# Grouped-query attention: stacked bf16 scores on the whole array against float32r scores in four row tiles

## The reference

```python
q = einsum('bsd,ed->bse', x, Wq).reshape(b, s, 32, 8).transpose(0, 2, 1, 3)
k = einsum('bsd,ed->bse', x, Wk).reshape(b, s, 8, 8).transpose(0, 2, 1, 3)
v = einsum('bsd,ed->bse', x, Wv).reshape(b, s, 8, 8).transpose(0, 2, 1, 3)
q, k = _apply_rope(q, k, s)
scores = jnp.einsum('bkgqd,bkld->bkgql', qg, k) * SCALE     # 1024 x 1024 a head
attn = jax.nn.softmax(scores, axis=-1)
out = jnp.einsum('bkgql,bkld->bkgqd', attn, v)
return jnp.einsum('bsd,ed->bse', out, Wo)
```

## Time and profile before

| | |
|---|---|
| median of 3 runs | 4268.53 us (4267.6 to 4272.98) |
| the profiled execution's own time | 4277.08 us |
| its span from the first to the last instruction | 4275.2 us |
| busy in the span | PE 86%, PEld 65%, DVE 62%, ACT 55%, POOL 18% |
| mean granted clock of PE | 0.944 |

### The profile page before, as it was taken

One profiled execution on the slowest core, in us unless ns is written; L12 is line 12 of the kernel. 1 busy time (PEld: TensorE's weight loads), 2 busy tenths in 40 slices (PEclk: granted clock), 3 DMA queues, 4 the chain that ended last, 5 costly groups with the idle time before them and its releaser, 6 DMA issues. The chain is left out here.

```text
span 4275.2 us, 66025 instructions
## 1 busy us (share of the span) xinstructions
PE 3696.2 (86%) x22804; PEld 2783.1 (65%) x22804; DVE 2636.4 (62%) x5009; ACT 2338.6 (55%) x4937; POOL 762.4 (18%) x864
## 2 busy tenths in 40 slices
PE   7999999992969969658888888886989999999979
PEld 6999999991848858312222222234878888988967
DVE  5666666666336653357666676633378888888853
ACT  5777677773413324126666666652256666766632
POOL 2233433220003410100000000002022323232200
PEclk9999999995989989859999999997989999999989
DMA  1000000000000000020000000002011011101010
GB/s 57 21 21 11 21 21 21 21 1 30 0 17 2 0 3 0 16 54 9 15 15 15 15 8 15 15 3 103 4 51 40 26 40 36 33 33 41 26 60 20
DMA packets 24580, 100.25 MB, mean 23 GB/s; under 512 B 5316, under 2 KB 6084, under 8 KB 18036
## 3 DMA queue, kind: packets, MB, share of 16 engines
q1 hardware_dynamic: 24356, 97.25, 7.0%
HBM read 84.52 MB, written 12.32 MB: 23 GB/s over the span
## 5 line engine op out<-in xcount | busy, mean ns | idle before, releaser
L1420 ACT ACTIVATE ga5m_pr<-ga5m_E 128x512 f32<-128x512 f32 x1024 | 582.2, 596 | 309.5 <-PE ga5m_E L1342 301.1
L1435 DVE TENSOR_REDUCE ga5m_nm<-ga5m_M 128x1 f32<-128x1024 f32 x512 | 597.9, 1218 | 179.4 <-PE ga5m_M L1328 178.9
L352 POOL TENSOR_TENSOR all_X<-all_X,at_part 128x512 f32<-128x512 f32 x256 | 335.2, 1309 | 996.0 <-ACT at_part L532 996.0
L1342 PE MATMUL ga5m_E<-ga5m_Q,ga5m_K 128*128 128x512 bf16 x1024 | 390.3, 393 | 65.8 <-ACT ga5m_pr L1420 51.8
L1328 PE MATMUL ga5m_M<-ga5m_K,ga5m_Q 128*128 128x512 bf16 x1024 | 323.9, 400 | 127.9 <-DMA ga5m_Q<-in_zrows 70.7
L417 PE MATMUL at_A<-all_ident,at_prob 128*128 128x128 f32 x2304 | 340.3, 274 | 30.2 <-ACT at_prob L540 20.9
L1342 PEld LDWEIGHTS ga5m_E<-ga5m_Q,ga5m_K 128*128 128x128 bf16 x1024 | 97.5, 98 | 405.4 <-ACT ga5m_pr L1420 346.9
L417 PEld LDWEIGHTS at_A<-all_ident,at_prob 128*128 128x128 f32 x2304 | 265.1, 140 | 59.0 <-DVE at_q1l L600 25.5
L616 DVE TENSOR_TENSOR at_pT1l<-at_A,at_pT1h 128x512 fp32r<-128x512 f32 (+1 forms) x384 | 235.6, 641 | 64.7 <-ACT at_pT1h L521 58.1
L1355 PE MATMUL ga5m_O<-ga5m_pr,ga5m_Vu 128*32 128x512 f32 x2048 | 270.9, 607 | 0.0
L1328 PEld LDWEIGHTS ga5m_M<-ga5m_K,ga5m_Q 128*128 128x128 bf16 x1024 | 88.5, 99 | 273.6 <-DVE ga5m_nm L1435 133.8
(11 more groups left out here) (328 smaller groups left out, 10660.7 us busy)
## 6 DMA issues: line engine op xcount, KB each, us to landing
at_raw<-in_pack SPq DMA_DIRECT2D x32, 1027.0 KB, 5.6
at_slope<-in_slopes SPq DMA_DIRECT2D x32, 512.0 KB, 4.1
ga5m_Q<-ga_qs SPq DMA_DIRECT2D x48, 192.0 KB
ga_qs<-ga5s_part SPq DMA_DIRECT2D x6, 512.0 KB
ga5m_K<-ga_ks SPq DMA_DIRECT2D x48, 48.0 KB
all_X<-in_x SPq DMA_DIRECT2D x1, 2048.0 KB, 7.2
tq_raw<-in_gu SPq DMA_DIRECT2D x1, 2048.0 KB, 7.6
hw_wug<-in_ug SPq DMA_DIRECT2D x1, 2048.0 KB, 9.7
```

Of the source, the lines that this page charges most:

```text
L352: nc.gpsimd.tensor_tensor(X[:, t:t + 2, :], X[:, t:t + 2, :], part[(i - 1) % 2][:, :, :], ALU.add).then_inc(added, 1)
L1342: nc.tensor.matmul(Eb[e % 2][:, :], K[slot][:, kt * P:(kt + 1) * P], Q[slot][:, j * SEQ + qh * 512:j * SEQ + qh * 512 + 512], start=True, ...
L1420: nc.scalar.activation(pr[e % NR][:, :], Eb[e % 2][:, :], ACT.Exp, scale=scale).then_inc(e_done, 1)
L1435: nc.vector.tensor_reduce(nm[slot][:, k:k + 1], Mb[k % 2][:, :], AX.X, ALU.max, negate=True).then_inc(nm_done, 1)
```

## The change

Scores. A query and a key are held as two float32r parts, high and low. Three products (high by high, high by low, low by high) are stacked as 24 rows of the contraction, with two more rows for two parts of the maximum. Each head of a unit has its own 32 partitions (`32 * j`) in `Q` and `K`, so that its matmuls use a row tile of 32 x 128 of the array. `Q` is 1024 columns wide in place of 4096. A second copy `Qx` holds head `j + 2` in row tile `j`'s place, so that the two matmuls of a row score (keys 0 to 511 and 512 to 1023) stand in two different row tiles.

Order. Work goes by half units (32 of them, 512 queries each); a row item is placed at every second key score, 42 key scores ahead of its half's own first one; the maxima of a half are turned 10 key scores ahead of it (`LEAD`). `E` has three banks, a product with the values stands seven key scores behind, and the turned maxima and outputs use the banks of `M` in place of `T`. The program is written out without loops.

Transfers. All transfers of the main part are issued by POOL in place of SP: 12 a load (K, Q and Qx for each of four row tiles) and 8 for each half's maxima. `Vx` is read in place; the copy `Vu` on POOL and the zeroing of `Q` on DVE are gone. The split in `ga5s` has three casts and three subtractions in place of nine and six, and stores float32 in place of bf16.

```diff
-    qs = nc.dram_tensor(f"{name}_qs", (NKV * NQ, 3, HD, TOK), BF16, kind="Internal").ap()
-    ks = nc.dram_tensor(f"{name}_ks", (NKV, 3, HD, TOK), BF16, kind="Internal").ap()
+    qs = nc.dram_tensor(f"{name}_qs", (NKV * NQ, 3, HD, TOK), F32, kind="Internal").ap()
+    ks = nc.dram_tensor(f"{name}_ks", (NKV, 3, HD, TOK), F32, kind="Internal").ap()
...
+                    for i, (src, m, M) in enumerate(work):
+                        high, low = (part[i][x][0:M, :].bitcast(F32) for x in (0, 1))
+                        out = ks if i == 1 else qs[m * 16:(m + 1) * 16]
+                        sp.wait_ge(cast_done, i + 1)
+                        sp.dma_start(out[:, 0], high).then_inc(stored, 16)
+                        sp.dma_start(out[:, 2] if i == 1 else out[:, 1], high).then_inc(stored, 16)
+                        sp.wait_ge(low_done, i + 1)
+                        sp.dma_start(out[:, 1] if i == 1 else out[:, 2], low).then_inc(stored, 16)
...
-            Eb = [s.ps(f"E{i}", [P, 512]) for i in range(2)]
+            Eb = s.ps("E", [P, 3, 512])
...
-            M_AT = [0, 0, 3, 2, 3, 2, 3, 2, 3, 3, 3, 3, 3, 2, 0, 0]
-            T_AT = 14
...
+            for h in range(NH):
+                first = PER * (h - 1) - LEAD
+                for r in range(4 * NQ):
+                    at_step.setdefault(first + 2 * r, []).append(("row", h, r))
+                at_step.setdefault(first + PER, []).insert(0, ("max", h, 0))
+                at_step.setdefault(PER * (h + 1) + 9, []).append(("out", h, 0))
...
+                def load(n):
+                    b, kv = divmod(n, NKV)
+                    cols = slice(b * SEQ, (b + 1) * SEQ)
+                    for j in range(NQ):
+                        rows = slice(32 * j, 32 * j + NROW)
+                        pool.dma_start(K[n % 2][rows, :],
+                                     ks[kv, :, :, cols].rearrange("a d n -> (a d) n")).then_inc(q_in[n % 2], 16)
...
+                def maxima(h):
+                    n, _, _, qh = place(h)
+                    pool.wait_ge(split_done, 2 * h + 2)
+                    for x in range(2):
+                        for j in range(NQ):
+                            row = 32 * j + NROW + x
+                            pool.dma_start(Q[n % 2][row:row + 1, qh * 512:(qh + 1) * 512].rearrange("o (a n) -> o a n", n=P),
+                                         mpart[x][4 * j:4 * j + 4, :]).then_inc(max_in, 16)
+
+                load(0)
+                load(1)
+                for h in range(NH):
+                    n, _, _, qh = place(h)
+                    maxima(h)
+                    if qh == 0 and 1 <= n < NUNIT - 1:
+                        pool.wait_ge(s_done, group_of[h * PER - 1] + 1)
+                        load(n + 1)
...
+                    if kind == "row":
+                        j, a = divmod(r, 4)
+                        q0 = qh * 512 + a * P
+                        if qh == 0 and r == 0:
+                            pe.wait_ge(q_in[n % 2], 16 * 12 * (n // 2 + 1))
+                        for x, (g, src) in enumerate(((j, Q), ((j + 2) % NQ, Qx))):
+                            rows = slice(32 * g, 32 * g + NROW)
+                            mm = nc.tensor.matmul(out[:, x * 512:(x + 1) * 512], src[n % 2][rows, q0:q0 + P],
+                                                  K[n % 2][rows, x * 512:(x + 1) * 512], start=True, stop=True)
+                    elif kind == "max":
+                        pe.wait_ge(m_read, no["row", h, 4 * NQ - 1] + 1)
+                        mm = nc.tensor.transpose(out[0:4 * NQ, 0:P], nm[h % 2][:, :], consts["ident"][:, :])
...
+                def key_scores(g):
+                    if g >= 3:
+                        pe.wait_ge(e_done, g - 2)
+                    for e in range(*groups[g]):
+                        h, k = divmod(e, PER)
+                        kt, j = divmod(k, NQ)
+                        n, b, kv, qh = place(h)
+                        if k == 0:
+                            pe.wait_ge(max_in, 16 * 2 * NQ * (h + 1))
+                        rows = slice(32 * j, 32 * j + NROW + 2)
+                        mm = nc.tensor.matmul(Eb[:, e % 3, :], K[n % 2][rows, kt * P:(kt + 1) * P],
+                                              Q[n % 2][rows, qh * 512:(qh + 1) * 512], start=True, stop=True)
+                    mm.then_inc(s_done, 1)
...
+                for t in range(START, END):
+                    if 0 <= t < NE and groups[group_of[t]][0] == t:
+                        key_scores(group_of[t])
+                    for x in at_step.get(t, []):
+                        item(x)
+                    if 0 <= t - 7 < NE and (t - 7) % NQ == 0:
+                        values((t - 7) // NQ)
...
+                    if b >= PER * (copied + 1) + 7 and copied < NH - 1:
+                        copy_o(copied)
+                        copied += 1
```

More of the change, by code:

```diff
@@ L1185, in grouped_attention @@
             with Scope(nc, name + "s") as s:
[L1186 to L1190, removed]
+                part = [[s.sb(f"part{i}{x}", [P, TOK], F32R) for x in "hl"] for i in range(3)]
+                cast_done, low_done, stored = s.sem("cast"), s.sem("low"), s.sem("stored")
                 block = s.block()
-                work = [(qf, 0, P), (qf, 1, P), (kf, 0, 64)]
+                work = [(qf, 0, P), (kf, 0, 64), (qf, 1, P)]
@@ L1194, in _ @@
                 @block.scalar
                 def _(act):
[L1196 to L1201, removed]
+                    for i, (src, m, M) in enumerate(work):
+                        nc.scalar.activation(part[i][0][0:M, :], src[0:M, m, :], ACT.Copy).then_inc(cast_done, 1)
@@ L1203, in _ @@
                 @block.vector
                 def _(dve):
[L1205 to L1210, removed]
+                    for i, (src, m, M) in enumerate(work):
+                        dve.wait_ge(cast_done, i + 1)
+                        nc.vector.tensor_tensor(part[i][1][0:M, :], src[0:M, m, :],
+                                                part[i][0][0:M, :].bitcast(F32), ALU.subtract).then_inc(low_done, 1)
@@ L1219, in _ @@
                     sp.wait_ge(stored, 16 * 9)
         with Scope(nc, name + "m") as s:
[L1222 to L1229, removed]
+            NH = 2 * NUNIT
@@ new lines, in grouped_attention @@
+            at_step = {}
+            for h in range(NH):
[4 more added lines that the diff above has]
+                at_step.setdefault(PER * (h + 1) + 9, []).append(("out", h, 0))
+            START, END = min(at_step), max(at_step) + 1
+            items = [x for t in range(START, END) for x in at_step.get(t, [])]
@@ L1388, in _ @@
-                pe.wait_ge(fixed_in, 32)
-                for k in range(NM):
-                    row_scores(0, 0, k)
-                turn_maxima(0, 0)
-                unit(0, 0, True, first=True)
-                unit(0, 1, True)
-                with pe.Fori(1, NUNIT // 2 - 1) as i:
-                    unit(i, 0, True)
-                    unit(i, 1, True)
-                unit(NUNIT // 2 - 1, 0, True)
-                unit(NUNIT // 2 - 1, 1, False)
-                turn_out(NUNIT - 1, 1, False)
+                pe.wait_ge(ones_in, 16 * 2 * NQ)
@@ L1411, in _, with copy_o @@
[L1411 to L1424 removed]
+                def copy_o(h):
+                    act.wait_ge(pv_done, QT * (h + 1))
+                    if h >= 1:
+                        act.wait_ge(m_done, no["out", h - 1, 0] + 1)
+                    nc.scalar.activation(Ot[:, :], Ob[:, :], ACT.Copy).then_inc(o_out, 1)
```

290 lines of the change are left out of this document (91 added, 199 removed).

## The result

The changed kernel takes 4446.2 us (median of 4 runs, 4442.48 to 4449.59) against 4269.02 us in the same session (4 runs, 4267.6 to 4272.98): a ratio of 1.0413, 95% interval 1.0395 to 1.0431. It is 4.1% slower. Forecast were 4160 us and a range of 4030 to 4320. The profiled execution has a span of 4445.4 us, and the mean granted clock fell from 0.944 to 0.826.

The account below looks back on a forecast made before the run. The prediction held that PE, DVE and ACT wait for each other, none being full. Halves falling from 29.6 to 26.3 us put the last key score at 2751, 108.5 us less: 4160 us, range 4030 to 4320.

Parts of the forecast that it names:

- A step after the change: Main loop, four key scores, two row items, one O: 2.34 (DVE) to 2.85 us, middle 2.60; PE's sum 2.41 to 2.85.
- The granted clock may fall in the waits: Remark among the expected profile signs: PE's clock might drop while it waits; no size given.
- I am wrong if the step itself is above 3 us: Stated sign of failure: a main-loop step of four exponentials, expected at 2.3 to 2.9 us, lasting over 3 us.
- the forecast's chain for a half: Half unit: 22 steps at 0.65, output, copy and reduction waits, then maxima turned, issued by POOL and landed: 26.3 us.
- Row tiles: Score matmuls in different row groups may run at once; a row-score pair costs PE 0.44 us overlapped, 0.88 if not.
- rival C: Row tiles don't overlap and shape changes around E, M and O cost more: step 3.1, result 4245 us; chance 0.10.
- POOL's transfers: Eight maxima transfers before each half's first key score, 0.9 us an issue, PE waiting about 3 to 4 us each half.
- rival A: POOL issues as fast as SP, 0.56 us: half 23.6, result 4067, or 4024 at DVE's bound; chance 0.23.
- Rival B: POOL's issue is dearer than about 1.3 us, so the gain is gone; at 1.5, result 4359 us; chance 0.22.
- The last reduction: Before the maxima are turned, PE waits for DVE's last row reduction: 0.3 us a half.
- copy of O: PE's first O of a half waits for ACT's copy of the previous output: 1.1 us a half.
- The start: Doubled stores at about 235 GB/s end at 1868, twenty POOL issues take 18 us, first key score at 1917.

Follow-up runs that it names:

- e8: The changed kernel with three order numbers altered (lead 12 in place of 10, maxima turned one exponential later, output copied after exponential 5), rows still 24 and 26: 4419.97 us.
- e4: The changed kernel with a zero-padded Q tile per head, no Qx, and both row and key scores contracting 64 rows: 4140.63 us.
- e6: The changed kernel with a zero-padded Q tile per head, no Qx, key scores contracting 128 rows and row scores 24: 4645.86 us.
- e3: The kernel before, with its bf16 score matmuls contracting only rows 0 to 23 of the stack (results not valid): 4761.49 us.
- h4: e4 with three order numbers altered (lead 12 in place of 10, maxima turned one exponential later, output copied after exponential 5): 4084.64 us.
- e2: The changed kernel with forty float32 matmuls of 128 rows put ahead of the stage's wait for its first loads: 4446.22 us.
- e7: The changed kernel with a zero-padded Q tile per head, no Qx, key scores contracting 26 rows and row scores 128: 4861.79 us.

## Why the prediction was wrong

**The step that failed** is the price of PE in "A step after the change": "a matmul of 512 columns takes 0.22 us". The row was read at a granted clock of 1.00, with 128 rows in every matmul, and I carried it to matmuls of 24 and 26 rows as if the clock were a constant. It was not among the bounds: the range of the step, 2.41 to 2.85, had no end at half the clock, nor did a rival. The clock is named once, in "The granted clock may fall in the waits", without a price, and e8, whose waits are gone and whose clock is still 0.50, does not bear that cause out. "I am wrong if the step itself is above 3 us" is what happened.

**Its size.** With POOL's measured issue of 0.52 us in place of 0.9, the forecast's chain for a half is 14.3 + 0.5 + 1.1 + 0.3 + 1.0 + 8 x 0.52 + 1.9 = 23.3 us. Without a wait for the maxima, which is what was measured, its own terms give 32 x 0.65 + 0.5 + 1.1 + 0.3 = 22.7 (the prediction adds 2.2 for the last three, which are 1.9, and says 23.0). Measured: 35.2, which is 12.5 more, and the step explains 8 x (4.06 - 2.60) = 11.7 of it. The last key score stands at 3027.3, 276 us behind the 2751 of the forecast. 31 halves of 8.9 us more than the forecast's 26.3 are 276 as well, but that the two agree is luck: the last half, forecast at 18.5, kept the step of 4.06, and the first key score came 15.6 us early, and these two nearly cancel.

**The step of 2.60 us** was met at the full clock by other tiles than forecast: 64 rows (e4) gave 2.61. The 2.60 was the middle between two bounds, so this is in part luck, and no run shows the forecast's own tiles at 1.00.

**Row tiles** do overlap, so the first half of rival C is refuted; its second, a price for a change of shape, is real between score matmuls of different extent (e6), which the changed kernel has only around O. "TensorE: Matmul & The Clock Gate", Part 3, of the Trainium skill gives 3.07x for four of them, and the trace agrees roughly: four matmuls go by in the 0.59 us from 2301.48 to 2302.07, where e3 at the same clock takes 0.43 for each (two row scores fill 2200.63 to 2201.49), 1.72 for four: 2.9x. Over the whole step the gain is smaller: eight score matmuls in 2.20 us, where 8 x 0.43 is 3.44, or 1.6x.

**The clock and how busy PE is.** PE was 93% busy in the steady part and got 1.2 GHz. The same page of the Trainium skill, Part 1, ties the clock gate to how busy PE is; by that rule the clock would have been 1.00 and the step about the 2.61 us of e4. The measurement decides.

**POOL's transfers** (the term said to decide) cost 0.52 us an issue, rival A's price. PE waited for them once, 1.0 us. At half the clock the ten key scores of lead last 10 us, which would hide even 0.9. At the full clock e4 still shows only 4 such waits on PE, 3.0 us in all, so rival A had this term right. Rival B did not come about: the POOL operation on 512 columns (1.26 us) was no guide to a POOL transfer, and neither was the 1.0 us that the prediction tried as a price of an issue.

**The last reduction** was put at 0.3 us a half. At the full clock (e4) PE waited for it 32 times, 37.9 us in all, 1.2 each; so this term was mis-sized too. The **copy of O** was put at 1.1, and there PE waited 31 times, 33.3 us in all, 1.1 each, as forecast. In the changed kernel, at half the clock, it was 33.1 in 32 and 21.1 in 31. PE's weight loads, which run ahead, wait longer; both waits of e4's weight loads from 1900 to 2700, with total, times and longest:

```profile
PEld ga5m_M L1317 <- DVE ga5m_nm L1395: 51.1, 32, 2.1
PEld ga5m_O L1347 <- ACT ga5m_Ot L1366: 44.7, 30, 1.5
```

They were on the path: with both nearly gone h4 is 56 us faster than e4 (one run each), a half falling from 25.3 to 23.5 us (key scores 1912.0 to 2664.8). At half the clock the same edit gave 26 (e8).

**The start** came early: first key score at 1901.4, not 1917. The stores moved 338 GB/s from 1835 to 1850 (223 in the same stretch of before, 235 in the forecast), POOL began at 1861.8, not 1868, and twenty issues at 0.52 save 7.6 of the 18 forecast:

```profile
1835.00:1850.00 15.00, 0.00 (x0) 0.00 (x0) 4.68 (x3) 1.55 (x1) 0.00 (x0) 0.50 0.97 338
```

Doubled bytes did not cost double time: the rate of one stretch of before was no limit. What held it there is not shown; DVE and ACT, which make the parts, were busy 13.07 and 14.42 of those 15 us before, and 4.68 and 1.55 after.

**Left open.** Where between 26 and 64 rows the clock comes back, and whether it is the 24 to 26 rows or the row tile of 32 that counts (the two were never apart). In the changed kernel the products O contract 128 rows (and fill 32 columns each) for 1.86 of 4.06 us, which does not raise the clock, while behind 16 of them in a row it rises (3028 in the changed kernel, 2183 in e3). Whether few-row matmuls also bring down a clock that is up: in e2 and e3 it was up when they began, but PE waited in between, and e8, which hardly waits, entered at 0.50. No run entered the steady part warm and without a wait. How a mixture of row counts sets the clock: e6 and e7 show only that it swings. The rows summed over a step do not order the runs: e6's eight score matmuls contract 4 x 128 + 4 x 24 = 608 rows and e4's 8 x 64 = 512, and e6 stood at 0.50 from 2300 to 2400 where e4 had 0.97.

## What to carry to other kernels

A price read at one granted clock holds only for matmuls that keep that clock: before a matmul is narrowed to few rows, ask what TensorE's clock does, and read the granted clock of the stage first when a kernel got slower. Four row tiles of 24 to 26 rows cost more here (step 4.06 us) than two halves of 64 rows filled with zeros (2.61), and changing the row count from matmul to matmul cost 0.2 us each time. An order that keeps the next work ahead of each wait (three banks, maxima half a unit ahead, turned behind a fresh row score) was worth 3.4% with full rows, 4.2% when tuned, and 4.7% when tuned and with 64-row halves.
